# Attention block with routed and shared feed-forward on one core: the opening, blocks 1, 2 and 12 to 15 and the passage to the experts are put in another order

## What is computed

```
q, k, v = silu(x @ Wq), silu(x @ Wk), x @ Wv          # 16 heads of 8
q, k = [t*cos(theta*n), t*sin(theta*n)] of each        # n: place in the sequence
out = ((q @ k.T) * tril) @ v                           # no softmax
out = layernorm((out @ Wo) * sigmoid(x @ G1 @ G2)) * gamma + beta
x1 = layernorm(x + out)
p, i = top_2(softmax(rmsnorm(x1) @ router_w.T))        # 8 experts, 1280 rows each at most
routed = scatter_add(w * (silu(xg @ rg) * (xg @ ru)) @ rd)
shared = (silu(x1 @ sg) * (x1 @ su)) @ sd
out = layernorm(x1 + shared + routed)
```

## Time and profile before

| | |
|---|---|
| median of 3 runs | 874.49 us (874.35 to 877.4) |
| the profiled execution: its time | 880.28 us |
| its span, first to last instruction | 878.5 us |
| PE busy | 824.7 us, 94% of the span |
| DVE, ACT, POOL busy | 611.4, 355.6, 391.6 us |
| mean granted clock of TensorE | 0.96 |

### The profile page before, as it was taken

The page is one execution under the profiler, slowest core; times in us unless marked ns, Lnnn a source line. Parts: engine busy times, 40 slices in busy tenths (PEclk is TensorE's granted clock), DMA queues, the critical chain, the costliest instruction groups (busy, mean ns, idle before and its releaser), DMA issues. The chain is left out here.

```text
span 878.5 us, 27876 instructions
## 1 busy us (share of the span) xinstructions
PE 824.7 (94%) x11178; PEld 671.8 (76%) x11178; DVE 611.4 (70%) x1945; ACT 355.6 (40%) x744; POOL 391.6 (45%) x363
## 2 busy tenths in 40 slices
PE   5898999999999999999998987899999999999995
PEld 3576777777777777777776756678999999998875
DVE  6455979789797887979788678774444544443665
ACT  6323544545354454544533233122333333322576
POOL 3502132424334143322425344375278777776433
PEclk9957999999999999999999789989999999999998
DMA  4514111111121111112121212032255545433544
GB/s 133 165 34 148 29 39 47 51 41 44 42 51 39 41 49 45 42 39 50 45 66 45 52 45 51 5 97 75 79 97 98 97 94 94 63 49 31 123 147 141
DMA packets 74480, 59.89 MB, mean 68 GB/s; under 512 B 10164, under 2 KB 64235, under 8 KB 74353
## 3 DMA queue, kind: packets, MB, share of 16 engines
q1 hardware_dynamic: 57584, 42.10, 17.1%
q0 software_dynamic: 16768, 16.01, 10.0%
HBM read 23.99 MB, written 28.89 MB: 60 GB/s over the span
## 5 line engine op out<-in xcount | busy, mean ns | idle before, releaser
L533 POOL DMA_INDIRECT dispatched_rows<-x,slot x128 | 131.7, 1029 | 209.7 <-PE energy_banks L1683 117.4
L644 POOL DMA_INDIRECT summed_rows<-VP,goal_i x80 | 123.7, 1546 | 43.0 <-issue 24.8
L964 ACT ACTIVATE sq<-energy_banks 128x512 f32<-128x512 f32 (+1 forms) x96 | 50.5, 526 | 120.1 <-PE energy_banks L1626 118.8
L1118 DVE TENSOR_TENSOR sf<-sf,bank 128x512 f32<-128x512 f32 x88 | 60.3, 685 | 41.1 <-PE bank L1626 39.8
L596 POOL TENSOR_TENSOR rr<-vq,minus_half 128x8 f32<-128x8 f32 x16 | 26.7, 1667 | 114.9 <-DVE vq L1188 114.8
L716 ACT ACTIVATE hidden_rounded<-sf 128x512 fp32r<-128x512 f32 x88 | 55.5, 630 | 37.3 <-DVE sf L1118 37.2
L1090 DVE TENSOR_TENSOR EM<-energy_and_gate_banks,causal 128x512 f32<-128x512 f32 x64 | 44.0, 687 | 36.0 <-PE energy_banks L1706 34.0
L706 ACT ACTIVATE sf<-energy_and_gate_banks 128x512 f32<-128x512 f32 x88 | 52.6, 598 | 37.2 <-PE energy_and_gate_banks L1626 34.1
L1726 PEld LDWEIGHTS bank<-VP,Kt 64*64 64x64 f32 x896 | 37.0, 141 | 30.9 <-issue 18.1
L1726 PE MATMUL bank<-VP,Kt 64*64 64x64 f32 x896 | 53.0, 240 | 7.1 <-DVE SM L1099 6.9
L679 ACT ACTIVATE sq<-bank 128x512 f32<-128x512 f32 x64 | 38.3, 598 | 49.2 <-PE bank L1626 45.4
(11 more groups left out here) (238 smaller groups left out, 2279.5 us busy)
## 6 DMA issues: line engine op xcount, KB each, us to landing
QM<-QT SPq DMA_DIRECT2D x256, 32.0 KB, 2.0
dispatched_rows<-empty POOLq DMA_DIRECT2D x8, 655.0 KB
QM<-dispatched_rows SPq DMA_DIRECT2D x8, 655.0 KB, 5.9
xin<-in_x SPq DMA_DIRECT2D x16, 256.0 KB, 2.9
QM<-summed_rows SPq DMA_DIRECT2D x16, 256.0 KB, 2.9
out_x<-QM SPq DMA_DIRECT2D x16, 256.0 KB, 3.2
summed_rows<-empty SPq DMA_DIRECT2D x13, 256.0 KB, 2.1
dispatched_rows<-x,slot POOLq DMA_INDIRECT x128
```

What stands on the lines that cost most here:

```text
L533: g.indirect_dma_start(out=xg_d, out_offset=bass.IndirectOffsetOnAxis(ap=slot[:, n % 2, j:j + 1], axis=0), in_=x1[:, n % 2, j % NC, :], in ...
L644: g.indirect_dma_start(out=sum_d, out_offset=bass.IndirectOffsetOnAxis(ap=goal_i[:, par, t:t + 1], axis=0), in_=ye[:, par, t, :], in_offse ...
L964: a.activation(sq[:, f % 2, 0:w], EB[f % 2][:, 0:w], ACT.Silu).then_inc(e_silu, 1)
L1118: v.tensor_tensor(sf[:, n % SF], sf[:, n % SF], UB[:], ALU.mult).then_inc(v_h, 1)
```

## The change

It moves work and adds none to speak of.

- **Opening.** DVE's low part of the q and k weights, its low part of the v weights, and one of the two products of each half of the sine table go to POOL. Of the 16 loads of `QM` for block 0, POOL issues eight and SP eight. ACT's clearing of half of tile `VP` and its copy `before` go into block 0.
- **Fills.** Of the eight DMAs that fill `dispatched_rows`, four were issued in block 0 and four in block 1, each time once that block's own loads of q had landed. Now two are issued in block 1 and six in block 2, with the same rule.
- **Blocks 1 and 2.** DVE does `second_moments` and `mean_square` ahead of the last `mask`; `scale_x1` of block 1's rows stands ahead of block 2's first `mask`.
- **Blocks 12 to 15.** In block 12 `project_out` goes ahead of the second energies, `gate_norm` ahead of the second mask and `two_best` ahead of the third. Blocks 13 and 14 get an order of their own: `mask(0)` comes before the low parts and `scale_x1`, `turn_x1` after the second energies, and both norms ahead of the second `shared_hidden`. Block 15 has `mask(0)` early in the same way, and its `slots` moves behind the block.
- **Passage.** Pairs 0 and 1 stand ahead of `turn_x1(B)` and four pairs, not two, ahead of `positions(B)`; `spread_down` is cut in three, with `positions(B + 1)` after its first quarter; `shared_add(SPARE, ...)` goes from between pairs 1 and 2 to between pairs 5 and 6.

The core of the diff (ACT's order, which follows PE's, and the semaphore names are left out):

```diff
+            return P * b + P // 2 if b >= 0 else 0
+        def q_by_head(eng, par, g2, h, loaded):
+            rows = slice(16 * h, 16 * h + 16)
+            eng.dma_start(QM[rows, g2, :, :, h % 2].rearrange("p t c n -> p (t c) n"),
+                          QT[rows, par, g2].rearrange("p t (c n) -> p (t c) n", c=2)).then_inc(loaded, 16)
...
-                        for h in range(8):
-                            rows = slice(16 * h, 16 * h + 16)
-                            sp.dma_start(QM[rows, g2, :, :, h % 2].rearrange("p t c n -> p (t c) n"),
-                                         QT[rows, 1 - par, g2].rearrange("p t (c n) -> p (t c) n", c=2)).then_inc(g_qm[g2], 16)
+                        for h in range(4 if b == -1 else 8):
+                            q_by_head(sp, 1 - par, g2, h, g_qm[g2])
...
-            gp.wait_ge(v_qk, 4)
+            gp.wait_ge(ld_q, 16)
+            gp.wait_ge(a_wq, 1)
+            g.tensor_tensor(wqk_lo, sq[:, 0], wqk_hi.bitcast(f32), ALU.subtract).then_inc(v_wq, 1)
...
+            gp.wait_ge(c_sin, 1)
+            for i in (0, 1):
+                g.tensor_tensor(products[:, i], coarse[1][:, i], fine[0][:, i], ALU.mult).then_inc(g_prod, 1)
+            gp.wait_ge(a_wvg, 1)
+            g.tensor_tensor(wvg_lo, wvg_s, wvg_hi.bitcast(f32), ALU.subtract).then_inc(v_wvg, 1)
+            gp.wait_ge(z_qm, 1)
+            gp.wait_ge(v_qk, 2)
+            for g2 in (0, 1):
+                for h in range(4, 8):
+                    q_by_head(gp, 0, g2, h, g_q0[g2])
...
+                if b in (1, 2):
+                    gp.wait_ge(c_pool, 23)
+                    gp.wait_ge(g_qm[1], loads_of_q(b))
+                    for e in (range(2) if b == 1 else range(2, E)):
+                        gp.dma_start(xg_r[e], empty[:]).then_inc(g_sc, 16)
...
-                if b in (0, 1):
-                    gp.wait_ge(c_pool, 23)
-                    gp.wait_ge(g_qm[1], P * (b + 1))
-                    for e in range(b * E // 2, (b + 1) * E // 2):
-                        gp.dma_start(xg_r[e], empty[:]).then_inc(g_sc, 16)
...
-                    clear(VP[:, 1].rearrange("p c n -> p (c n)"), 4 * 512).then_inc(z_vp, 1)
-                    act.wait_ge(c_pool, 21)
-                    a.activation(before[:], before_f, ACT.Copy).then_inc(a_bf, 1)
-                    act.wait_ge(z_vp, 2)
+                    act.wait_ge(z_vp, 1)
...
-            dve.wait_ge(ld_q, 16)
-            dve.wait_ge(a_wq, 1)
-            v.tensor_tensor(wqk_lo, sq[:, 0], wqk_hi.bitcast(f32), ALU.subtract).then_inc(v_wq, 1)
...
-            def table_half(i):
-                link(v.tensor_tensor(by_place[:, i], coarse[0][:, i], fine[1][:, i], ALU.mult))
-                link(v.tensor_tensor(products[:, i], coarse[1][:, i], fine[0][:, i], ALU.mult))
+            def table_sum(i):
+                need(dve, g_prod, i + 1)
                 link(v.tensor_tensor(table[:, i], table[:, i], KT[:, 0, i], ALU.add))
...
-                    table_half(0)
+                    for i in (0, 1):
+                        link(v.tensor_tensor(by_place[:, i], coarse[0][:, i], fine[1][:, i], ALU.mult))
+                    table_sum(0)
                     turn(f, fp, 0)
-                    wvg_low()
-                    table_half(1)
+                    table_sum(1)
...
-                    mask_state(b, 6)
                     if back:
                         centre(b)
                         add_input(b)
-                    mask(b, par, 3)
+                    mask_state(b, 6)
                     if back:
                         second_moments(b)
                         mean_square(b)
+                    mask(b, par, 3)
                 def with_feed_forward():
...
                             hidden_lo(b - 1, f7)
                     input_lo()
+                    if shared_turn(b - 1) is None:
+                        scale_x1(b - 1, par)
                     mask(b, par, 0)
                     mask_state(b, 1)
                     if shared_turn(b - 1) is not None:
                         slots(b - 1, 1 - par)
-                    else:
-                        scale_x1(b - 1, par)
...
+                    else:
+                        input_lo()
+                        mask(b, par, 0)
+                        mask_state(b, 1)
                         hidden_lo(b - 1, spare_turn(b - 1, 1), SPARE)
                         scale_x1(b - 1, par)
+                        mask_state(b, 2)
                         shared_hidden(b, s0, SPARE)
+                        turn(f, fp, 0)
+                        mask(b, par, 1)
+                        mask_state(b, 3)
+                        gate_norm(b)
+                        hidden_lo(b, s0, SPARE)
+                        gate_moments(b)
+                        mask_state(b, 4)
+                        turn(f, fp, 1)
+                        copy_logits(b)
+                        turn(f, fp, 2)
+                        mask(b, par, 2)
+                        mask_state(b, 5)
+                        centre(b)
+                        add_input(b)
+                        two_best(b)
+                        choices(b, par)
+                        turn(f, fp, 3)
+                        mask_state(b, 6)
+                        second_moments(b)
+                        mean_square(b)
+                        shared_hidden(b, s1, SPARE)
+                        mask(b, par, 3)
+                        read_positions(b)
+                    slots(b, par)
...
+                def last_block():
+                    s0, s1 = spare_turn(b, 0), spare_turn(b, 1)
+                    mask_state(b, 0)
                     mask(b, par, 0)
                     mask_state(b, 1)
...
                     hidden_lo(b - 1, spare_turn(b - 1, 1), SPARE)
+                    shared_hidden(b, s0, SPARE)
                     scale_x1(b - 1, par)
-                    shared_hidden(b, s0, SPARE)
-                    mask(b, par, 0)
-                    mask_state(b, 1)
                     mask_state(b, 2)
                     gate_norm(b)
-                    gate_moments(b)
                     shared_hidden(b, s1, SPARE)
                     mask(b, par, 1)
                     mask_state(b, 3)
+                    gate_moments(b)
                     hidden_lo(b, s0, SPARE)
...
+            rows_lo(RELOADED)
+            slots(B - 1, 1)
+            gate_norm(B)
             scale_x1(B - 1, 0)
-            rows_lo(RELOADED)
-            gate_norm(B)
+            spread_hidden(RELOADED, 0)
             gate_moments(B)
-            spread_hidden(RELOADED, 0)
+            spread_hidden(RELOADED, 1)
             copy_logits(B)
             two_best(B)
             choices(B, 0)
-            spread_hidden(RELOADED, 1)
+            spread_hidden(RELOADED, 2)
             centre(B)
             add_input(B)
+            spread_hidden(RELOADED, 3)
+            read_positions(B)
             second_moments(B)
             mean_square(B)
+            slots(B, 0)
+            spread_hidden(RELOADED, 4)
+            spread_hidden(RELOADED, 5)
+            scale_x1(B, 1)
             dve.wait_ge(m_x1[0], 16)
             shared_add(SPARE, x1t[:, 0], PB[0])
-            spread_hidden(RELOADED, 2)
-            read_positions(B)
-            slots(B, 0)
-            spread_hidden(RELOADED, 3)
-            spread_hidden(RELOADED, 4)
-            scale_x1(B, 1)
-            spread_hidden(RELOADED, 5)
             spread_hidden(RELOADED, 6)
...
+                    else:
+                        states_and_out(1)
+                        project_out(b)
+                        energies_and_state(1)
+                        turn_x1(b, par)
+                        states_and_out(2)
+                        project(f, 1)
+                        project(f, 2)
+                        logits(b)
+                        energies_and_state(2)
+                        project(f, 3)
+                        values_projected(0)
+                        states_and_out(3)
+                        values_projected(1)
...
+                    shared_pair(s1, SPARE)
                     turn_x1(b, par)
-                    shared_pair(s1, SPARE)
...
+            spread_pair(RELOADED, 0)
+            spread_pair(RELOADED, 1)
             turn_x1(B, 0)
-            spread_pair(RELOADED, 0)
+            spread_pair(RELOADED, 2)
             logits(B)
-            spread_pair(RELOADED, 1)
+            spread_pair(RELOADED, 3)
             positions(B)
             down_back(SPARE, PB[0])
-            for f in range(2, 6):
-                spread_pair(RELOADED, f)
+            spread_pair(RELOADED, 4)
+            spread_pair(RELOADED, 5)
             turn_x1(B + 1, 1)
             spread_pair(RELOADED, 6)
+            logits(B + 1)
             spread_pair(RELOADED, 7)
-            logits(B + 1)
-            spread_down(RELOADED, (0, 1))
+            spread_down(RELOADED, (0,))
             positions(B + 1)
```

(1 more changed line is left out.)

175 lines of the change are left out of this document (93 added, 82 removed).

## The result

The changed kernel takes 866.27 us (median of 4 runs, 862.77 to 869.19) against 875.94 us (4 runs, 874.35 to 882.47). The ratio is 0.989, with a 95% interval of 0.985 to 0.993: some 10 us faster, where 20 were forecast. Two later sets of runs gave 0.989 (0.983 to 0.995) and 0.986 (0.981 to 0.991). In the sets of e17 and e18 two executions lie far off the rest (1096 and 2535 us), so I give their medians too, and e2's profiled execution (897.58 us, median of its runs 889.45) was a slow one, so its rows are not used.

What follows compares the result with a forecast made beforehand. PE was taken as the bound (824.7 of 878.5 us busy), through waits and the clock falls behind them, with DVE second. Terms summed to -20.1 us: 860.2 for the profiled execution, 854 for the median; 8-in-10 range 842 to 868.

Steps and rivals of the forecast that it cites:

- opening: Before block 0: earlier silu and shorter DVE list, partly lost to POOL and DVE overlaps; -1.0 us, bounds -1.6 and +0.5.
- fill wait and block 1's clock: Start of block 1: PE's 2.62 us wait behind the fills goes, -2.6 us; the clock then stays full, -7.0.
- from block 1 to block 2: Block boundary: the wait for scale_x1 goes, -2.1 us, and less time at the low clock, -0.9; together -3.
- blocks 12 to 15: Late blocks: shorter waits and less low clock; -0.5 us in block 12, -4 in 13 and 14, -4 in 15.
- passage: After block 15: spread_down waits for a later load of sd; +2 us, bounds -1 and +4.
- Block 1's clock: Block 1: without the wait, the 20.48 us at clock 0.50 become 13.5; -7.0 us, bounds -10.2 and 0.
- the wide range, 842 to 868: Whole kernel: 8-in-10 range, taking in rivals with clock kept or lost in block 1, and unknown prices.
- the rival that had 862: Block 1: the clock falls all the same, the rest is reached in part; -12 us, 862 us, chance 22%.
- The exclusion: Opening: DVE with two SBUF inputs and POOL reading SBUF shut each other out; DVE 3.1 us later if always.
- the -0.9 for a shorter low stretch: Block 1 to block 2: less time at the low clock; -0.9 us, bounds 0 and -4.
- the late load of `sd`: Passage: sd, issued behind the moved shared_add, lands at 592.2 us, PE needs it at 589.8; +2.4, taken as +2.
- the 6.13 us wait (about 5): Passage: PE arrives sooner and waits about 5 us at turn_x1(B + 1); scale_x1 ends within 0.5 us of before.

Runs made afterwards that it cites:

- e17: Changed kernel with the whole opening of before (low parts and products on DVE, q loads by SP, clearing in the opening): ratio 0.988, medians 863.75 to 874.67.
- e18: Kernel before with the new fills, the new order of norms and scale_x1 in blocks 1 and 2, and of blocks 12 to 15: ratio 0.988, medians 863.6 to 874.67.
- e2: Changed kernel with the fills back in blocks 0 and 1 (four and four): ratio 1.002 to the kernel before.
- e1: Kernel before with only the fills moved to blocks 1 and 2 (two and six): ratio 0.996.
- e4: Changed kernel with the old order of norms and scale_x1 in blocks 1 and 2: ratio 0.997 to the kernel before.
- e14: Changed kernel with the fills back in blocks 0 and 1, on the same chip as the changed kernel: ratio 0.995 to the kernel before.
- e7: Changed kernel with the old order of blocks 12 to 15 on all engines: ratio 1.000 to the kernel before.
- e10: Kernel before with the new order of blocks 12 to 15 alone: ratio 0.989.
- e6: Kernel before, unchanged, for a second profile of its stages: one execution at 870.61 us.
- e5: Changed kernel itself, run again for its time and stages: ratio 0.989 to the kernel before.
- e13: Changed kernel itself, run again as the reference on one chip: ratio 0.986 to the kernel before.
- e16: Changed kernel with the passage of before, on the same chip as the changed kernel: ratio 0.984 to the kernel before.
- e15: Changed kernel with the old places of norms and scale_x1 in blocks 1 and 2, same chip as the changed kernel: ratio 0.992 to the kernel before.
- e11: Changed kernel with the opening's computations on DVE and POOL's memset behind the turned q and k: ratio 0.988 to the kernel before.
- e9: Changed kernel with the passage of before: ratio 0.983 to the kernel before, median 859.86 us.
- e3: Changed kernel with the opening's low parts and second sine products back on DVE, POOL's memset left early: ratio 0.996 to the kernel before.

## Why the prediction was wrong

The mechanisms named were mostly there; the sum was twice the gain. Term by term, forecast and what the stages show (means over profiles with and without the part, e1 to e4 left out):

| term | forecast | shown |
|---|---|---|
| opening | -1.0 | +0.2 (20.3 to 20.5 us) |
| fill wait and block 1's clock | -9.6 | -4.6; by e1 -4, by e14 -7 |
| from block 1 to block 2 | -3.0 | -2.1 |
| blocks 12 to 15 | -8.5 | -7.9 (117.7 to 109.8 us); by e7 and e10 -10 |
| passage | +2.0 | +3.7 |
| sum | -20.1 | -10.7 |

**The step that failed is "Block 1's clock", -7.0.** It priced the 20.48 us at the low clock that stood in one trace. e6 and e10, with the same fills and a wait at the same place (1.79 and 2.79 us), had 3.4 and 6.8 us of it. The bounds I gave (-10.2 to 0) held the truth, and I took a value near the one trace. That is half of the missing 10 us. The profiled execution, 880.28 us, lay 5.8 us above the median of its runs, and I carried the sum over to the median unchanged. What an unusually slow execution loses to the clock can't be won back from a usual one. Between the two profiled executions themselves block 1 went from 29.3 to 20.4 us: 2.6 by the wait and 6.3 by the clock, close to the 7.0. So the step was right for that trace and wrong for the median to which it was carried. The measured 866 us lies in the wide range, 842 to 868, but not by the rival that had 862: in the three profiles of the changed kernel the clock didn't fall in block 1.

**The opening.** The exclusion was named, with the sum it would give (3.1 us late, nothing left), and then taken at -1.0. The rows after come to the same sum: 1.65 and 0.42 us lost by DVE on products and sum, and 0.98 ahead of them (2.12 us for three steps of the angles, 1.14 before). That it is 3.05 and the forecast 3.1 is partly luck: products and sum lost less than thought, and the loss on the angles was not among the overlaps named. The second `values_projected` step came at 17.05 us, where 15 to 16 were forecast. The rule of the Trainium skill ("SBUF — State Buffer", Who interferes with whom) gave 0, and it was right over my value.

**Block 1 to block 2.** The wait for a mask came as forecast (1.88 us), none for `scale_x1`, and the clock fell for 10.24 us, as long as before: the -0.9 for a shorter low stretch did not come in this profile.

**Blocks 12 to 15.** Right in size and mostly in detail: no wait above 0.87 and 0.72 us in the first halves, 1.80 and 1.68 us before `positions` (forecast 1.9), no wait of 3 us in block 15. Block 12's wait shrank from 1.81 to 0.89 us, but the block took 31.5 us and not 30.8, 3.4 of them at the low clock. e7 and e10 show that this part carries the change.

**The passage.** The direction and the cause, the late load of `sd`, were right; the size was too small. In the first profile its wait is missing, since the low clock (0.50 throughout) made pairs 6 and 7 last 1.0 us beyond the landing. It is there in the two others of the changed kernel, 1.04 us in e5 and this in e13, where 2 were forecast:

```profile
566.50 1.12 PE L2038 MATMUL bank<-ident,x 128*128 128x128 f32 x4 [6.13 <-DVE x L1170]
569.15 0.38 SPq L420 DMA_DIRECT2D EM<-in_sd  x1
573.52 2.02 PE L2115 MATMUL bank<-EM,he 128*128 128x128 f32 x16 [1.21 <-DMA EM<-in_sd]
```

From `turn_x1(B + 1)` to this `spread_down` it is 7.02 us in e13 and 4.43 in e16. In six of the eight profiles with the new passage (e5, e7, e13, e14, e15, e17) `spread_down` starts within 0.15 us of the landing of `sd`; in the other two, the first and e11, at the low clock, 1.0 to 1.1 us after it. With the old passage `sd` had landed 2.3 to 3.0 us before it was needed. So the landing costs 2.6 us here, near the +2.4 of the sum. This is read from the stages; no run moves the load of `sd` alone. The visible wait is shorter because pairs 6 and 7 ran partly at the lower clock, a mean of 0.72 in e13; that clock costs something only where it outlasts the landing.

What the sum had at nothing is the rest. I had named the 6.13 us wait (about 5), with `scale_x1(B, 1)` no later because DVE's list was as long as before. It comes 0.8 us later after the first turn back than in e16 (20.8 us to `turn_x1(B + 1)` against 20.0). 0.8 and 2.6 are the 3.4 us between e13 and e16.

The last stage took 75.3 us in the two profiles of before and 76.5 in the three of the changed kernel; nothing in the change touches it, and I have not found out why.

## What to carry to other kernels

Before pricing a clock's fall from one trace, look how that execution's time stands to the others, and if it is slower, price the stretch with the shorter ones that the same trace shows behind like waits. Work moved to an idle engine is only free if that engine doesn't shut out the busy one, and pushing it later may only move the collision. Before moving an instruction past others in a queue, follow not only who waits for it but who waits for the ones it overtakes.

## What the runs showed of the hardware

The length of a low stretch behind a wait at the same place differs from one execution to the next: 3.41, 6.83 and 20.48 us in block 1 with the old fills (waits of 1.79, 2.79 and 2.62 us). Behind block 2's first wait it was 10.24 us in the first profile of the changed kernel (wait 1.88 us), 3.41 in e5 and e13 (2.45 and 1.85), and the clock didn't fall at all in e9 (1.60). Block 0's clock was 0.99 or 1.00 in 14 of 19 profiles, and in e7 and e14 it was at 0.59 on average with no wait of PE over 1.4 us there.

POOL's memset, which reads no SBUF, stood beside a DVE instruction with one SBUF tile as input that took 1.32 us instead of 0.26 (e3). In the changed kernel two SCALAR_TENSOR_TENSOR steps beside the same memset took 0.36 us each, as without it.

In the executions of e1 to e4 small matmuls followed each other more slowly. The groups view of `attend`'s matmuls, before and then e1, busy us and mean ns:

```profile
L1683 PE MATMUL energy_banks<-EM,VP 64*32 64x64 f32 x4096 | 57.5, 233 | 0.0
```

```profile
L1684 PE MATMUL energy_banks<-EM,VP 64*32 64x64 f32 x4096 | 63.3, 230 | 0.4 <-issue 0.2
```

One takes as long as before, but a block's 256 of them take 4.0 to 4.4 us in blocks 3 to 11 of e1, where most blocks of e6 take 3.4. The runs of before had a median of 886.9 us there, and 874.7 to 876.6 in the other sets. What sets these executions apart is not known.
